# Two message-passing layers on one core: moving five buffers of the edge stage to one stretch at the top of SBUF

## The reference, cut to what matters

```python
# layer 0: one three-layer perceptron over every edge, used in both directions
inp  = concat([x[f], x[t], edge_attr])              # 384 wide
h    = relu(relu(inp @ w1.T + b1) @ w2.T + b2)      # 256 wide
msg  = h @ w3.T + b3                                # 128 wide
agg  = segment_sum(msg(src, dst), dst) + segment_sum(msg(dst, src), src)
s    = three GRU cells over (x, agg)
x    = layernorm(x + s)
# layer 1, three times: sum over neighbours, two 128x128 products
X    = relu(((1 + eps) * X + segment_sum(X[src], dst)) @ W1 + b1) @ W2 + b2
out  = layernorm(x + X)
```

## Time and profile before

| | |
|---|---|
| median of three runs | 2313.74 us (2311.68 to 2316.02) |
| profiled execution, its own time | 2316.54 us |
| its span, first to last instruction | 2314.8 us |
| busy: PE, DVE, ACT, POOL | 98%, 76%, 53%, 51% |
| granted TensorE clock, mean | 0.994 |
| DMA, mean rate over the span | 126 GB/s |

### The profile page before, as it was taken

The page is one execution under the profiler, slowest core; times in us unless marked ns, Lnnn a source line. Parts: engine busy times, 40 slices in busy tenths (PEclk is TensorE's granted clock), DMA queues, the critical chain, the costliest instruction groups (busy, mean ns, idle before and its releaser), DMA issues.

```text
span 2314.8 us, 38789 instructions
## 1 busy us (share of the span) xinstructions
PE 2257.0 (98%) x12559; PEld 1831.4 (79%) x12559; DVE 1762.0 (76%) x4035; ACT 1231.7 (53%) x2118; POOL 1182.7 (51%) x858
## 2 busy tenths in 40 slices
PE   4999999999999999999999999999999999899997
PEld 3888888888888888888888888888888874587775
DVE  7888888888888888888888888888888856703112
ACT  4565666566666656665666566656656543411122
POOL 2566666666566656665666666666656640001100
PEclk9999999999999999999999999999999999999999
DMA  4356454455445554554554445444545339286965
GB/s 163 71 113 125 98 106 92 88 112 101 91 89 106 99 98 91 108 97 89 100 112 93 88 98 107 99 89 104 101 89 99 72 62 268 94 351 258 384 263 189
DMA packets 242547, 292.52 MB, mean 126 GB/s; under 512 B 126757, under 2 KB 200056, under 8 KB 234385
## 3 DMA queue, kind: packets, MB, share of 16 engines
q1 hardware_dynamic: 168194, 236.50, 33.9%
q0 software_dynamic: 73216, 54.58, 18.0%
q10 hardware_dynamic: 1040, 0.52, 0.1%
HBM read 218.43 MB, written 73.08 MB: 126 GB/s over the span
## 4 chain that ended last, share of the span: by engine, by line
PE 92%; DMA 3%; DVE 2%; issue 1%; ACT 1%; POOL 0%; DVEq 0%; SPq 0%; POOLq 0%; ACTq 0%
PE bank L1238 24%; PE bank L1224 18%; PE bank L1250 16%; PE bank L2136 8%; PE bank L1303 4%; PE bank L1282 4%; PE bank L1298 4%; PE bank L1185 4%; DMA l_ring<-adj 2%; PE bank L1801 2%; PE bank L1267 2%; PE bank L1809 1%; PE bank L1268 1%; PE bank L2150 1%; PE bank L2159 1%
## 5 line engine op out<-in xcount | busy, mean ns | idle before, releaser
L495 POOL DMA_INDIRECT sums<-outb,target x416 | 667.3, 1604 | 590.8 <-ACT outb L666 456.8
L488 POOL DMA_INDIRECT xg<-in_x,gidx x416 | 489.3, 1176 | 148.3 <-issue 137.1
L1250 PEld LDWEIGHTS bank<-w3t,h 128*128 128x128 f32 x3328 | 387.5, 192 | 8.8 <-issue 0.2
L1250 PE MATMUL bank<-w3t,h 128*128 128x128 f32 x3328 | 388.3, 275 | 0.1
L1238 PE MATMUL bank<-h1h,w2h 128*128 128x512 f32 x832 | 365.5, 439 | 3.3 <-DVE h1l L861 3.3
L648 ACT ACTIVATE h<-bank,b2c 128x512 f32<-128x512 f32 x416 | 286.2, 688 | 122.2 <-PE bank L1238 122.2
L634 ACT ACTIVATE h1h<-hpre 128x512 fp32r<-128x512 f32 x416 | 257.8, 628 | 171.9 <-DVE hpre L857 171.9
L1238 PE MATMUL bank<-h1h,w2l 128*128 128x512 f32 x832 | 328.8, 395 | 0.0
L1238 PE MATMUL bank<-h1l,w2h 128*128 128x512 f32 x832 | 328.5, 395 | 0.0
L861 DVE SCALAR_TENSOR_TENSOR h1l<-hpre,h1h 128x512 fp32r<-128x512 f32 x416 | 268.6, 687 | 16.8 <-ACT h1h L634 16.8
L857 DVE TENSOR_TENSOR hpre<-pb,bank 128x512 f32<-128x512 f32 x416 | 264.9, 676 | 2.3 <-PE bank L1224 2.1
(11 more groups left out here) (263 smaller groups left out, 3695.6 us busy)
## 6 DMA issues: line engine op xcount, KB each, us to landing
l_ring<-adj SPq DMA_DIRECT2D x54, 1568.0 KB, 8.2
rowb<-along SPq DMA_DIRECT2D x104, 512.0 KB, 4.4
ef<-in_edge_attr SPq DMA_DIRECT2D x103, 256.0 KB, 2.7
adj<-band SPq DMA_DIRECT2D x46, 480.0 KB
adj<-band SPq DMA_DIRECT2D x23, 540.0 KB
stay<-adj SPq DMA_DIRECT2D x6, 1568.0 KB, 14.8
xg<-in_x,gidx POOLq DMA_INDIRECT x416
sums<-outb,target POOLq DMA_INDIRECT x416, 4.0
```

The costliest lines, as they stand in the source:

```text
L488: pool.indirect_dma_start(out=to, out_offset=None, in_=a["x"], in_offset=bass.IndirectOffsetOnAxis(ap=ids, axis=0)).then_inc(s_x[par], 16)
L495: pool.indirect_dma_start(out=tables[k % 2], out_offset=bass.IndirectOffsetOnAxis(ap=target[par][:, 1, k:k + 1], axis=0), in_=outb[par][:, ...
L1250: last = nc.tensor.matmul(bank[6 + way][:, t * P:(t + 1) * P], h2[:, way, k, t * P:(t + 1) * P], w3t[:, k, :], start=not bias and k == 0, ...
```

## The change

The order of the `sb(...)` lines is changed, and nothing else: no instruction, wait, queue, size or loop differs. `sdl`, `h1h` and `h1l` move from the middle of the list to its end, behind `sdh` and `hpre`; the small buffers `lower` to `blkkey` move from the end to a place ahead of `band`.

```diff
@@ edge_stage
         hot = sb("hot", [P, GE], f32r)
-        sdl = sb("sdl", [P, 3, GE], f32r)
         pb = sb("pb", [P, HB, GE])
-        h1h = sb("h1h", [P, 2, HB, GE], f32r)
-        h1l = sb("h1l", [P, 2, HB, GE], f32r)
         h2 = sb("h2", [P, 2, HB, GE])
         es = sb("es", [P, 2, GE])
         match = sb("match", [P, K, P])
         found = sb("found", [P, 4, K])
         shift = sb("shift", [P, 3, K])
-        band = sb("band", [P, NB * BAND])
-        target = [sb(f"target{i}", [P, 3, K], i32) for i in range(2)]
-        outb = [sb(f"outb{i}", [P, K, D]) for i in range(2)]
-        sdh = sb("sdh", [P, 3, GE], f32r)
-        hpre = sb("hpre", [P, HB, 2, GE])
-        b3r = sb("b3r", [P, D])
-        indegs = sb("indegs", [P, PACE])
-        fits = sb("fits", [1, 1], i32)
-        outdegs = sb("outdegs", [NB, P])
         lower = sb("lower", [P, P])
         column = sb("column", [P, P])
         spots = sb("spots", [P, GE], f16)
...
         blkkey = sb("blkkey", [P, G, K])
+        band = sb("band", [P, NB * BAND])
+        target = [sb(f"target{i}", [P, 3, K], i32) for i in range(2)]
+        outb = [sb(f"outb{i}", [P, K, D]) for i in range(2)]
+        b3r = sb("b3r", [P, D])
+        indegs = sb("indegs", [P, PACE])
+        fits = sb("fits", [1, 1], i32)
+        outdegs = sb("outdegs", [NB, P])
+        sdh = sb("sdh", [P, 3, GE], f32r)
+        hpre = sb("hpre", [P, HB, 2, GE])
+        sdl = sb("sdl", [P, 3, GE], f32r)
+        h1h = sb("h1h", [P, 2, HB, GE], f32r)
+        h1l = sb("h1l", [P, 2, HB, GE], f32r)
```

## The result

Twelve runs of each kernel on the same chips give medians of 2313.18 us before and 2316.99 us after, a ratio of 1.0017 with a 95% interval of 1.0009 to 1.0024. That is 0.17%, and the interval excludes 1: the change makes the kernel a little slower. The profiled execution of the changed kernel took 2320.44 us around a span of 2318.6 (before: 2316.54 and 2314.8).

What follows compares the result with a forecast made beforehand. The prediction took PE, never idle in the edge stage, as the bound: its instruction count times the distance between matmul starts. Terms 0 + 0 + 0 + 0.3 us on the median of 2313.74 gave 2314.0 us, range 2304 to 2323.

Steps and rivals of the forecast that it cites:

- PE bounds the edge stage, and waits for nothing: Edge stage, 100 to 1880 us: PE busy 1779.28 of 1780 us, three waits of 0.7 us together.
- No other engine changes, and it wouldn't matter: DVE and ACT on moved buffers: 0 us, `h1l` stays at 685 ns; slower operations have 1.35 or 0.51 us of cover.
- The home of an operand does not change the step: Both layers' 4368 matmuls on moved operands keep 0.232 us each: 0 us, 8.7 us allowed to either side.
- named as a sign: First layer in the changed kernel's profile: ten matmul steps should still take 2.32 us.
- The three tests: Equal step for `sdh` and `sdl`, equal step in the second layer, 2.99 us for first and last `stay` panel.
- the bound: Whole kernel: the measurement tells about 0.2%, 4.6 us, from no change; chance of staying within it 0.67.
- freed stream: Both layers: PE's reads, no longer disturbed by neighbouring buffers, gain 8.7 us, to 2305 us; chance 0.16.
- crowded stretch: Both layers: accesses falling into 36864 bytes hold engines up, 2323 to 2336 us; chance 0.12.
- late adds of `outb`: Behind the last group: two accumulating adds in series land late, 8.2 us more, 2322 us; chance 0.05.
- 0.3 us for them in the sum: Behind the last group: two `outb` landings in series, each taken as 0.15 us longer.
- The stand of PE at line 1809: Behind the last group: PE's stand of 0.78 us near 1906.89 should stay under 1 us.

Runs made afterwards that it cites:

- e3: Changed kernel with 32 bytes of padding ahead of `sdh` alone; 2309.47 us, ratio 0.9981 to the kernel before.
- e9: Changed kernel with 64 bytes of padding ahead of `w1h` and 32 ahead of `sdh`; ratio 0.9976 to the kernel before.
- e4: Kernel before with 32 bytes of padding ahead of `sdl` and 32 behind `h1l`; 2309.69 us, ratio 0.9983.
- e11: Kernel before with 32 bytes of padding ahead of `sdl` and 96 behind `h1l`; 2310.67 us, ratio 0.9986.
- e1: Kernel before with 32 bytes of padding ahead of `sdh` and 32 behind `hpre`; ratio 1.0014 to the kernel before.
- e7: Changed kernel with 96 bytes of padding ahead of `sdh`; 2317.34 us.
- e6: Kernel before with 32 bytes of padding ahead of `xw` and 32 ahead of `outb`; ratio 0.9999.

## Why the prediction was right, and where its argument wasn't

- *PE bounds the edge stage, and waits for nothing.* Right: 1779.57 of 1780 us busy, two waits of 0.5 us together. Not in that view are the 2 us of pauses in the first layer, the same before and after. It is why the 0.0016 us of a step reach the total at all.
- *No other engine changes, and it wouldn't matter.* Right: 685 and 685 ns became 684 and 684.
- *The home of an operand does not change the step; 0, with 0.002 x 4368 = 8.7 us allowed to either side.* Ten first-layer steps took 2.34 us, not the 2.32 that were named as a sign. The size held (+0.0016 in one layer, +1.9 us for the loop; the best homes give -6.5 us), but the statement was wrong, and this is the step that failed. The three tests behind it could not see the effect. The panels of `stay` lie 12800 bytes apart, 100 x 128, so the first and the last have the same distance from any weights within 128 bytes: the test varied the home by 64000 bytes and held fixed the one thing on which the later runs turn. (The last panel also covers under half of the new `h1l`, 3872 of 8192 bytes, and not most of it.) And the equal 0.232 us of the two layers came from different distances, 64 and 32 in the first layer and 32 in the second; their means are 0.2316 and 0.2327, rounded alike by a listing in hundredths.
- *The time came out within the bound partly by luck.* The change took `sdh` alone from a distance of 64 to 32 and left the three others at 32, among the slow ones in either kernel. With 32 bytes of padding more (e3) the same crowded layout takes 2309.5 us in place of 2317.0, and the prediction had no term that could tell the two apart.
- *Rival: freed stream, faster.* Not seen. Crowded e3 and e9 are as fast as e4 and e11, which are spread out.
- *Rival: crowded stretch, slower.* The sign came true, the mechanism didn't: e1 has the slowdown without the crowd, e9 has the crowd and is the fastest.
- *Rival: late adds of `outb`, and 0.3 us for them in the sum.* The landing has a median of 4.2 us before and 4.7 in e1, both with `outb` on a multiple of 256 bytes, and 4.3 in e3 and 4.0 in e4, both 64 past one. No dearer start shows. The trace of the changed kernel has no landing times for `outb`, but the waits at the end that the 0.3 us stood for: 0.73 + 0.71 = 1.44 us, where the earlier trace rows have 0.58 + 0.85 = 1.43. So the 0.3 us was a term for nothing. By the rule in the Trainium skill, "DMA: Bandwidth & Descriptors", "How a descriptor splits into AXI transactions", e3 and e4 should have had the longer ones; these runs don't resolve it.

```profile
1898.46 1.55 POOL L495 DMA_INDIRECT sums<-outb,target  x1 [0.73 <-DMA sums<-outb,target]
1900.72 1.55 POOL L495 DMA_INDIRECT sums<-outb,target  x1 [0.71 <-DMA sums<-outb,target]
```

- The stand of PE at line 1809 is 0.78 us in both kernels, as foretold.
- The 2.0 us at the start and the 1.7 us behind the last group had no step in the prediction, which took the clock as given. A change that alters no instruction went with 3.1 to 3.6 us more of the lower level at each end.

The Trainium skill, "SBUF — State Buffer", "Who interferes with whom", says that PE never waits for anyone. For the other engines as a cause the runs agree: crowding cost nothing. But the rule is about one engine waiting for another. The prediction took it as agreeing with a step that no home changes, and the step went from 0.2290 to 0.2333 us by homes alone; the measurement decides.

## What to carry to other kernels

Where PE is never idle, read the distance between the starts of its matmuls, since busy time cannot show that it slows down: the four windows above are all over 99.9% busy and differ by up to 40 instructions. Listed lengths and rows in hundredths of a microsecond are too coarse for this: average over many turns. Try a few paddings of 32 to 96 bytes between the weights and what is streamed past them, and measure each; here a distance of 64 was best and equal alignment of everything among the worst. e9 is 0.24% faster than the kernel before (0.13 to 0.34%), for two lines of padding. When a change of homes moves the total by a microsecond or two, look at the granted clock at the ends of the stage before the steps are blamed.

## What was not expected of the hardware

- A 512-column step of this kind took 0.2290 to 0.2333 us on average according to homes alone, 1.9%, at the full granted clock of 2.4 GHz. It is reproducible: 0.2316 and 0.2316 in two profiles of one program.
- The single steps follow patterns that repeat every two, three or six matmuls: 0.230 and 0.236 in turn in the first layer of e7; 0.229, 0.231, 0.226 in e3; 0.236, 0.229, 0.229, 0.227, 0.235, 0.232 before.
- One set of homes can run in two patterns from turn to turn (0.229 and 0.232 in e4 and e6).
- The clock's lower level at the start and behind the last group lasted some 7 us in some layouts and some 10 in others, the same in two profiles of one program.
